# Decoder layer on one core: another order of instructions in a head pass, and a first pass with a program of its own

## The reference

```python
# 1: attention, 32 query heads and 8 key/value heads of 128 channels, int4 weights with a scale per 128 rows
w = (qw.astype(f32) - 8) * repeat(scales, 128, axis=0)
q, k, v = x @ w_q, x @ w_k, x @ w_v
q, k = rope(q), rope(k)        # t * cos + rotate_half(t) * sin
attn = softmax(causal(q @ k.T / sqrt(128)))
y = (attn @ v) @ w_o
# 2: attention to ctx, 16 heads of 32 channels, softmax over axis 0 of (batch * heads)
# 3: dense layer plus a two-of-eight LoRA mixture, gated by a small network
```

## Time and profile before

| | |
|---|---|
| Median of three runs | 731.64 us |
| The profiled execution, its own time | 731.3 us |
| Its span | 729.5 us |
| Mean granted TensorE clock | 0.978 |
| TensorE busy | 660.2 us, 90% |
| VectorE busy | 556.2 us, 76% |
| ScalarE busy | 452.6 us, 62% |
| GpSimd busy | 433.6 us, 59% |
| Phase -1 (first matmul of pass 0 to that of pass 1) | 11.93 to 38.03 us |
| Phase 0 | 38.03 to 66.92 us |
| Phases 1 to 14 | 66.92 to 479.0 us, 28.8 to 31.0 us each |
| Phase 15 and the last outs | 479.0 to about 505.6 us, then the other sublayers |

### The profile page before, as it was taken

The page is one execution under the profiler, slowest core; times in us unless marked ns, Lnnn a source line. Parts: engine busy times, 40 slices in busy tenths (PEclk is TensorE's granted clock), DMA queues, the critical chain, the costliest instruction groups (busy, mean ns, idle before and its releaser), DMA issues. The chain is left out here.

```text
span 729.5 us, 10970 instructions
## 1 busy us (share of the span) xinstructions
PE 660.2 (90%) x3297; PEld 448.2 (61%) x3298; DVE 556.2 (76%) x864; ACT 452.6 (62%) x1252; POOL 433.6 (59%) x379
## 2 busy tenths in 40 slices
PE   3579989999999999999999999978999889969994
PEld 2355867777778677677677777754554443348541
DVE  5756989899899898898898989955360359998446
ACT  2248859769788797796986976966233555412100
POOL 3759778888988988987998898852220000012002
PEclk9989999999999999999999999999999999979997
DMA  8344651441351242243144123130010000020003
GB/s 291 95 133 123 195 151 44 116 131 41 96 140 44 76 147 54 69 135 86 44 122 110 45 73 87 38 138 0 1 57 1 1 1 1 0 91 2 0 1 115
DMA packets 29469, 56.46 MB, mean 77 GB/s; under 512 B 4705, under 2 KB 4961, under 8 KB 28898
## 3 DMA queue, kind: packets, MB, share of 16 engines
q1 hardware_dynamic: 29410, 55.76, 26.9%
HBM read 32.67 MB, written 2.10 MB: 48 GB/s over the span
## 5 line engine op out<-in xcount | busy, mean ns | idle before, releaser
L943 DVE SCALAR_TENSOR_TENSOR arena<-ps,arena 128x512 f32<-128x512 f32 x288 | 213.5, 746 | 42.3 <-PE ps L1250 28.7
L1250 PE MATMUL ps<-x_hi,w_sb 128*128 128x512 f32 x384 | 176.1, 459 | 27.8 <-DVE x_lo L925 19.4
L971 DVE SCALAR_TENSOR_TENSOR y<-ps,arena,y 128x512 f32<-128x512 f32 x192 | 138.3, 742 | 28.8 <-PE ps L1309 28.7
L1250 PE MATMUL ps<-x_lo,w_sb 128*128 128x512 f32 x384 | 152.6, 397 | 0.0
L668 ACT ACTIVATE arena<-ps,arena 128x512 f32<-128x512 f32 x96 | 67.6, 704 | 98.7 <-PE ps L1250 88.2
L1309 PE MATMUL ps<-heads_hi,wo_sb 128*128 128x512 f32 x256 | 115.4, 451 | 7.3 <-DVE arena L943 3.0
L558 POOL TENSOR_TENSOR y<-arena,y 128x512 f32<-128x512 f32 x64 | 82.2, 1285 | 63.6 <-ACT arena L718 60.4
L540 POOL TENSOR_TENSOR arena<-arena,consts 128x512 f32<-128x512 f32 x80 | 103.5, 1294 | 27.2 <-DMA arena<-arena 25.6
L1250 PEld LDWEIGHTS ps<-x_hi,w_sb 128*128 128x128 f32 x384 | 73.3, 191 | 70.5 <-issue 34.0
L534 POOL TENSOR_TENSOR arena<-arena,consts 128x512 f32<-128x512 f32 x80 | 104.0, 1300 | 7.8 <-DVE arena L943 7.2
L550 POOL TENSOR_TENSOR arena<-arena 128x512 f32<-128x512 f32 x80 | 103.4, 1293 | 5.8
(11 more groups left out here) (117 smaller groups left out, 948.1 us busy)
## 6 DMA issues: line engine op xcount, KB each, us to landing
arena<-arena SPq DMA_DIRECT2D x160, 128.0 KB, 2.3
arena<-in_qkv SPq DMA_DIRECT2D x48, 256.0 KB, 3.7
arena<-in_o SPq DMA_DIRECT2D x32, 256.0 KB, 3.8
arena<-in_x_t SPq DMA_DIRECT2D x8, 256.0 KB, 5.6
y<-in_x SPq DMA_DIRECT2D x4, 512.0 KB, 4.2
arena<-in_ctx_t SPq DMA_DIRECT2D x4, 512.0 KB, 5.8
out<-y SPq DMA_DIRECT2D x8, 256.0 KB, 2.2
arena<-in_wk SPq DMA_DIRECT2D x1, 1024.0 KB, 5.9
```

What stands on the lines that cost most here:

```text
L943: nc.vector.scalar_tensor_tensor(acc, product_bank(f"G{KC * c + g}"), scale_of(p // 2, c, g), acc, ALU.mult, ALU.add).then_inc(dve_scaled, 1)
L971: nc.vector.scalar_tensor_tensor(dst, by_tile(out_bank(p, u)), out_scale_of(p // 2, u), dst, ALU.mult, ALU.add).then_inc(out_added, 1)
L1250: mm = nc.tensor.matmul(product_bank(f"G{u}"), w_sb[:, c, g, :], part[:, g, half * HALF:(half + 1) * HALF], start=(k == 0), stop=(k == 1))
```

## The change

1. **Order of a phase.** The lists of all four compute engines and `PRODUCTS` are rewritten. On TensorE O0 comes after three groups (six before), S0 after O0 and three more groups (and no longer after eight groups), V is after G2.2 (11th group), T0 before the tile 3 groups, S3 after T1, and the phase ends O13, O14, O15, W3 (before: O13, O14, W3, O15). VectorE's and ScalarE's lists follow. On GpSimd the weight conversions and outs lie elsewhere, and `cosine(2)` stands before `sine(2)`. The counts of operations stay the same.
2. **First pass.** x^T is loaded and cut chunk by chunk, each with its semaphore, and w tile 0 is loaded after chunk 0. ScalarE converts the first weights (before: GpSimd). ScalarE also makes `ident_b` and `mask_b` (before: VectorE, five small casts). The products of pass 0 go through seven banks in place of four. `raw_first`, `turned_first` and `cos_first` give every tile its own place (in the region of heads_hi and heads_lo), so no ring wait is left. VectorE's 18 additions go in the order `FIRST_SUMS`, which alternates tiles. Of the 15 rope operations GpSimd keeps eight and VectorE takes seven (sin and sum of tile 3, cos, sin and sum of tile 5, sin and sum of tile 4).
3. **Second half of x^T.** It is loaded after the turn of tile 0. VectorE makes its four x_lo between its last additions. ScalarE waits for `out_scales_in` only after phase 0.

```diff
@@ -52,8 +52,9 @@
 PRODUCTS = (
-    "G0 G1 G2 G3 G4 G5 O0 G6 G7 G8 O1 G9 G10 G11 O2 O3 G12 O4 O5 O6 G13 O7 G14 G15 G16 O8 O9 G17 O10 G18 G19 "
-    "G20 O11 O12 G21 G22 G23 O13 O14 O15").split()
+    "G0 G1 G2 O0 G3 G4 G5 G6 O1 G7 G8 G9 G10 G11 O2 O3 O4 O5 G12 O6 O7 O8 G13 G14 G15 O9 G16 G17 G18 G19 G20 "
+    "G21 O10 O11 G22 G23 O12 O13 O14 O15").split()
+FIRST_SUMS = "0.1 0.2 1.1 0.3 1.2 2.1 1.3 2.2 3.1 2.3 3.2 4.1 3.3 4.2 5.1 4.3 5.2 5.3".split()
 TURNS = "V T0 T1 T2 T3".split()
...
+        raw_first = carve(NT, HALF, base=HEADS_AT)
+        turned_first = carve(len(ROPE_TILES), HALF)
+        cos_first = carve(len(ROPE_TILES), HALF)
...
+        first_ps = [0, 1, 2, 7, 3, 4, 6]
...
+        def group_bank(p, u):
+            if p == 0:
+                return banks[first_ps[u % len(first_ps)]]
+            return product_bank(f"G{u}")
+        def raw_of(p, c):
+            return raw_first[:, c, :] if p == 0 else raw[:, c % RING, :]
+        def wait_group_read(eng, p, u):
...
+            def load_x(half, g):
+                sp.dma_start(x_stage[:, g, half * HALF:(half + 1) * HALF],
+                             t["x_t"][:, g, half * HALF:(half + 1) * HALF]).then_inc(x_in[half][g], 16)
+            def load_first_w(c):
+                sp.dma_start(w_int[:, c], t["qkv"][0][:, c]).then_inc(w_first_in[c], 16)
+            load_x(0, 0)
+            load_first_w(0)
+            for g in range(1, KC):
+                load_x(0, g)
             sp.dma_start(scales[:, :], t["qkv_scales"]).then_inc(scales_in, 16)
-            for c in range(1, NT):
-                sp.dma_start(w_int[:, c], t["qkv"][0][:, c]).then_inc(w_first_in[c], 16)
-                if c == 1:
-                    sp.dma_start(consts[:, :, :], t["consts"]).then_inc(consts_in, 16)
-            load_x(1)
+            load_first_w(1)
+            load_first_w(2)
+            sp.dma_start(consts[:, :, :], t["consts"]).then_inc(consts_in, 16)
+            for c in range(3, NT):
+                load_first_w(c)
...
-                    turn(p, c)
+            def turn_first(c):
+                wait(sp, dve_scaled, summed_count(0, c))
+                i = ROPE_TILES.index(c)
+                for a, b in ((0, 64), (64, 0)):
+                    sp.dma_start(turned_first[a:a + 64, i, :], raw_first[b:b + 64, c, :]).then_inc(first_turned_in[i], 16)
+            turn_first(0)
+            for g in range(KC):
+                load_x(1, g)
+            for c in ROPE_TILES[1:]:
+                turn_first(c)
             for k in range(QPK):
                 load_wo_piece(0, k)
...
@@ -588,19 +635,19 @@
                 cosine(0)
                 weights(0)
                 sine(0)
+                weights(1)
+                total(0)
+                cosine(2)
+                weights(2)
                 outs(3)
-                total(0)
                 sine(2)
-                cosine(2)
+                outs(7)
+                cosine(3)
                 total(2)
-                cosine(3)
-                outs(7)
-                weights(1)
+                weights(3)
                 sine(3)
                 total(3)
                 cosine(4)
-                weights(2)
-                weights(3)
                 sine(4)
                 cosine(5)
                 total(4)
@@ -608,14 +655,38 @@
                 total(5)
                 outs(11)
                 weights(4)
+                weights(5)
                 outs(15)
-                weights(5)
-            for c in range(NT):
-                wait(pool, w_first_in[c], 16)
-                convert(c)
             pool.wait_ge(consts_in, 16)
-            phase(-1)
...
+                nc.gpsimd.tensor_tensor(dst, cos_first[:, i, :], turned_first[:, i, :], ALU.add).then_inc(rotated, 1)
+            first_cos(0)
+            first_sin(0)
+            first_cos(2)
+            first_total(0)
+            first_sin(2)
+            first_cos(3)
+            first_total(2)
+            first_cos(4)
             phase(0)
...
+            def first_weights(c):
+                act.wait_ge(w_first_in[c], 16)
+                nc.scalar.activation(w_sb[:, c], w_int[:, c], ACT.Copy, bias=-ZERO).then_inc(w_ready, 1)
+            cut_x(0, 0)
+            first_weights(0)
+            for g in range(1, KC):
+                cut_x(0, g)
             act.wait_ge(scales_in, 16)
             def scale_group(p, c):
...
@@ -773,44 +850,62 @@
                 scale_groups(0)
                 scale_groups(1)
+                exp(0)
                 scale_groups(2)
-                exp(0)
-                exp(1)
                 seed(2)
                 norm(0)
+                copy_values()
+                exp(1)
                 outs(3)
+                seed(3)
+                copy_turned(0)
+                weights(0)
                 scale_groups(3)
-                copy_values()
-                seed(3)
+                outs(7)
+                exp(2)
                 norm(1)
-                copy_turned(0)
-                exp(2)
-                weights(0)
-                outs(7)
+                weights(1)
                 copy_head(0)
                 scale_groups(4)
+                norm(2)
+                seed(4)
                 copy_turned(1)
-                norm(2)
+                scale_groups(5)
                 exp(3)
                 copy_head(1)
                 copy_turned(2)
-                scale_groups(5)
+                norm(3)
                 outs(11)
-                norm(3)
+                weights(2)
                 copy_head(2)
-                seed(4)
                 copy_turned(3)
-                weights(1)
-                weights(2)
                 seed(5)
-                copy_head(3)
                 outs(15)
                 weights(3)
-            phase(-1)
-            cut_x(1)
+                copy_head(3)
+            first_weights(1)
+            scale_group(0, 0)
+            first_weights(2)
+            scale_group(0, 1)
+            act.wait_ge(consts_in, 16)
+            nc.scalar.activation(ident_b[:, :], ident, ACT.Copy).then_inc(mask_ready, 1)
+            first_weights(3)
+            scale_group(0, 2)
+            first_weights(4)
+            scale_group(0, 3)
+            first_weights(5)
+            copy_v(0)
+            scale_group(0, 4)
+            cut_x(1, 0)
+            cut_x(1, 1)
+            scale_group(0, 5)
+            cut_x(1, 2)
+            cut_x(1, 3)
+            nc.scalar.activation(mask_b[:, :, :], mask.unsqueeze(1).broadcast_to([P, QPK, P]), ACT.Copy).then_inc(mask_ready, 1)
+            phase(0)
             act.wait_ge(out_scales_in, 16)
-            for f in range(2 * NKV):
+            for f in range(1, 2 * NKV):
                 phase(f)
             act.wait_ge(params_in, 64)
...
@@ -996,41 +1087,79 @@
                     if f >= 0:
                         cut_heads(n + s)
-                add_groups(0, 1, 2, 3)
-                add_groups(1, 1, 2)
+                add_groups(0, 1, 2)
                 outs(0)
+                add_groups(0, 3)
+                add_groups(1, 1)
                 maximum(0)
+                add_groups(1, 2)
+                outs(1)
                 add_groups(1, 3)
+                inv(0)
                 maximum(1)
-                outs(1)
-                add_groups(2, 1)
-                inv(0)
-                add_groups(2, 2, 3)
+                add_groups(2, 1, 2, 3)
+                outs(2)
+                maximum(2)
+                outs(4, 5, 6)
                 inv(1)
-                outs(2, 4, 5, 6)
-                maximum(2)
+                outs(8)
                 add_groups(3, 1, 2)
-                maximum(3)
                 inv(2)
                 add_groups(3, 3)
+                outs(9)
                 cut(0)
-                outs(8)
                 add_groups(4, 1)
-                outs(9)
-                add_groups(4, 2)
+                maximum(3)
+                add_groups(4, 2, 3)
                 outs(10)
-                add_groups(4, 3)
+                add_groups(5, 1)
                 inv(3)
                 cut(1)
-                outs(12)
-                add_groups(5, 1, 2)
+                add_groups(5, 2, 3)
                 cut(2)
-                add_groups(5, 3)
-                outs(13, 14)
+                outs(12, 13, 14)
                 cut(3)
-            phase(-1)
-            cut_x(1)
...
+            for name in FIRST_SUMS[:13]:
+                first_sum(name)
+            cut_x(1, 0)
+            first_sum("4.2")
+            first_sum("5.1")
+            cut_x(1, 1)
+            first_sum("4.3")
+            first_sum("5.2")
+            cut_x(1, 2)
+            first_sum("5.3")
+            first_sin(3)
+            cut_x(1, 3)
+            first_total(3)
+            first_cos(5)
+            first_sin(4)
+            first_total(4)
+            first_sin(5)
+            first_total(5)
             phase(0)
             dve.wait_ge(y_in, 16 * BPH)
```

(69 more changed lines are left out.)

118 lines of the change are left out of this document (77 added, 41 removed).

## The result

The changed kernel takes 711.5 us (median of four runs, 709.9 to 712.4), and the kernel before took 731.8 us on the same chip: a ratio of 0.971, 95% interval 0.969 to 0.974. The prediction was 715.5 us, with a range of 702 to 726. The profiled execution took 712.35 us with a span of 710.6, so 18.9 us of span are to be found (729.5 - 710.6).

A forecast was written before the change was run, and what follows sets the result against it. TensorE was taken to bound a steady phase, the other engines close behind, with latencies setting phase 0. From 731.3 us, terms of -8, -1, -3.5, -2 and -1.5 gave 715.3, as a median 715.5 us; range 702 to 726.

The forecast's parts named there:

- term 1: First pass: VectorE's first addition of pass 1 starts near 34 against 42.07 us; -8.0 us, from -12 to 0.
- Rival A: First pass: all moved rope operations and x_lo collide with GpSimd's, so the start gains 0; 723.5 us, chance 0.15.
- term 2: Phase 0: GpSimd's chain some 2 us shorter, half of it counted; -1 us, from -2.5 to +1.
- Rival D: Start and steady phases: the early lead is lost before phase 1, phases keep their length; 731 +- 1 us, chance 0.03.
- term 3: Phases 1 to 14: fewer TensorE stalls, a mean gain of 0.25 us each; -3.5 us, from -15 to +7.
- small pieces: Steady phases: many small delays in TensorE's start times, some 0.5 us a phase, counted beside the named stalls.
- this walk: One steady phase of the new order followed by instruction distances: named stalls of 0.6 (odd) and 1.0 us (even).
- rival B: Phase boundary: W3 last puts W3, copy, cut and O0 across it, so O0 comes late; slower, 736 us, chance 0.09.
- Rival C: Steady phases: the new order fits far better than the walk, 1.0 us a phase; 705 us, chance 0.20.
- term 4: Single stalls of phases 2 and 10, 2.8 us: more than half goes; -2 us, from -3 to 0.
- term 5: Phase 15: the rope chain before its first scores starts 1.3 us earlier; -1.5 us, from -3 to +1.

The follow-up runs named there:

- d: The changed kernel with all 15 rope operations of the first pass on GpSimd: 712.7 us, ratio 0.972 to the kernel before.
- k: The changed kernel with 38 matmuls whose result nobody reads, placed where TensorE waits in phase 0: 709.2 us, ratio 0.970.
- l: The changed kernel with c, j, k (3 matmuls for 8 behind G3.0), late ctx loads, and odd phases' loads behind the last turn: 704.9 us.
- j: The changed kernel with head 1's weight loads issued between the turns of the first pass: 712.4 us, ratio 0.973.
- a: The changed kernel's first pass with the phase lists and product order of the kernel before: 723.2 us, ratio 0.987.
- c: The changed kernel with ScalarE reading G3.0 right after the second exponentials in phase 0: 710.0 us, ratio 0.970.
- h: The changed kernel with W3 back ahead of O15, and ScalarE's copy of heads 3 back ahead of out 15: 720.3 us, ratio 0.984.
- g: The kernel before with only O0 moved, behind three groups in place of six: 732.9 us, ratio 1.002.
- i: The changed kernel with S0 moved later, behind G1.3, and VectorE's maximum 0 and reciprocal moved to suit: 734.7 us, ratio 1.003.
- e1: The changed kernel with the four ctx loads issued near the end of the 16 passes: 708.9 us, ratio 0.970.
- b: The kernel before with the new phase lists and product order, its first pass otherwise as it was: 719.8 us, ratio 0.982.

## Why the prediction was right or wrong

**The start (term 1, -8.0; measured -8.9): right, by its mechanism.** The first addition was forecast near 10.3 and came at 10.21; the first of pass 1 near 34, and came at 33.18. Two errors offset each other in this: the thirteenth addition was over at 20.7 in place of 19.6, and two collisions in place of four gave back 2.1 us. The wait for the out scales is gone. (The 0.95 of phase -1, which I took for the slow first products, comes from its last 2.8 us; the slow start itself is there, in the distances.) Where two-input operations of both engines overlap they exclude each other (1.63 and 1.59 us from start to start against 0.75 and 0.6), as the Trainium skill says (SBUF — State Buffer, Who interferes with whom). Rival A took this rule as applying to all eleven; it needs both engines to be at it, and GpSimd had ended. Kernel d shows the other side: with the rope left to GpSimd, VectorE is free earlier and TensorE waits for GpSimd.

**Phase 0 (term 2, -1; measured +2.85): this step failed.** I reckoned with latencies of attention and rope that would stay or shrink. What I had not in the sum is the granted clock. Before, TensorE was at half clock from 35.2 and was back at full clock at 42.1, just when the first addition of pass 1 let it work. After, it works in spurts and the half clock lasts from 26.8 to 37.0, 3.9 us beyond the first addition, with another 3.4 us later. Kernels k and l show that this is the cause: at full clock the 24.85 us are back within 0.2. GpSimd's wait (j) is ruled out, and the new list adds at most 0.5 us (a). c, which only moves one read in ScalarE's list, gives back 1.7 us by itself and nothing on top of k: most of its gain, too, is a stretch of half clock that does not come. Rival D named the place (phase 1 no earlier than 60 us; it started at 60.87), but not this reason, and it held only for a third of the lead.

**The order of the phase (term 3, -3.5; measured about -11): right in sign, a term mis-sized threefold.** Undisturbed phases went from 29.25 to 28.0 us and from 28.8 to 28.5. The term that was mis-sized is what would be left of the stalls: I had 1.1 (odd) and 1.5 us (even), and what a phase takes beyond TensorE's own 27.45 is 0.55 and 1.05. O0 waiting for heads_lo, where I had 0.25 and 0.45 us and the traces show 0.17 and 0.19, is a smaller part of that; the rest is in the 0.5 us of small pieces and the bits at G1.1, W3 and O10. One reading in this walk was wrong, without weight: the W of the earlier trace rows ends at 185.42 and not at 185.26, so its copy follows after 0.03 us, not 0.2. The walk followed W3 to O0 as a risk, which rival B made its whole case. It did not follow what ScalarE does *while* W3 runs, nor how much longer an earlier W3 waits for its own input, and most of the gain needs these two: h, which undoes this alone, costs 1.1 us in odd phases, nearly the whole 1.25, and 0.5 in even ones, more than the 0.3. g shows that O0's place, my own reason, gives nothing by itself. The parts are not additive: i loses more than the whole gain by undoing S0's place alone. Rival C (1.0 us per phase) was the nearer for this term, which came out at 0.8. Rival B's sum leaves out my own gain of 3.5 us: the change would turn slower with O0 later by 16 / 14 = 1.14 us and not 0.9, and 1.2 us later gives 732.4, not 736.

**The single stalls (term 4, -2; measured about +2.3): this step failed.** I gave S0 a reserve of 1.1 us, with the last rope sum 2.6 us into the phase, and no loads in front of the turned tiles. In the kernel after this sum ends 3.1 to 3.2 us into the odd phases from 3 on. In even phases it ends at 3.8 and 3.9 us even where the tile is usable 3.2 and 3.3 us after its issue (phases 8 and 12), only 0.2 to 0.3 us ahead of S0. Where it takes 4.3 us (phases 4 and 10) it ends at 4.8, and with the ctx loads (phase 2) at 6.3. GpSimd in the kernel after, the last sums ahead of phases 4 and 8, which start at 149.35 and 263.83:

```profile
152.91 1.28 POOL L597 TENSOR_TENSOR arena<-arena 128x512 f32<-128x512 f32 x1
...
266.30 1.29 POOL L597 TENSOR_TENSOR arena<-arena 128x512 f32<-128x512 f32 x1
```

So S0 stalls 2.45, 0.64, 0.56 and 0.96 us in phases 2, 4, 6 and 10, where only 2 and 10 had a stall of their own before. For phase 2 e1 shows the cause, the ctx loads. For phases 4, 6 and 10 the cause beyond the thin reserve is open: transfers behind the same loads land at different times, from phase to phase and from run to run. That phase 2 grew more than its stall is again the clock (95.1 to 98.5 at half).

**Phase 15 (term 5, -1.5; measured -2.9): right, and larger.** The first scores of phase 15 in the kernel after, answering to the earlier trace rows:

```profile
466.12 1.13 PE L1397 MATMUL ps<-arena 128*128 128x128 f32 x8 [0.65 <-POOL arena L597]
```

They wait 0.65 us in place of 2.85; O0 ahead of them waits 1.4. The 1.3 us in the other two sublayers, which I had at 0, are most likely luck: the profiled execution after had 7.9 us at half clock there, the one before 21.9.

So two terms were too hopeful by 8 us together (2 and 4), and three too cautious by 10 (1, 3 and 5). That the total came within 4 us is in good part luck.

## What to carry to other kernels

An engine that is the bound can lose its clock while others catch up: when a change moves work of the others ahead, look where the bound engine idles in the new order, and price the same work at the lower clock (here 2.65 us of a lead of 8.9, given back in the trace by 38 matmuls that nobody reads). In lists that are taken in order, ask of each late instruction what its readers do while it runs, and what it waits for at the earlier place: W3 last gave ScalarE cover worth about 0.6 us in odd phases, and spared TensorE 0.3 to 0.5 us of waiting for W3's own input. Before an edit is credited with a stall that went away, look whether the stall is there in the other traces with the old code. A reserve that hangs on a small transfer is to be sized with the transfers ahead of it on its queue, and loads that nobody needs soon belong behind it.

## What the runs showed of the hardware that I had not expected

- The granted clock stays at 0.50 for 10.2 us (26.8 to 37.0) when TensorE works in spurts, 6.8 us in the kernel before, 13.7 in a, b, d and g. A stretch of 3.4 us of half clock came with single waits of 2.46 us (ending at 46.41) and 2.17 us (ending at 95.44).
- The two transfers of a turn (128 KB each, inside SBUF) are usable 2.9 us after their issue where no load was issued near them (the last turn ahead of phases 3 and 7), 3.2 to 4.3 us with two loads of 256 KB issued 2.2 to 2.8 us ahead and one behind, and 5.7 us with loads of 512 KB among them. One turn with two loads of 256 KB ahead took 3.1, so these loads don't always cost.
- A gain in the span of one profiled run may hardly show in the medians: c gained 3.6 us of span and 1.5 us of median, inside the intervals. Executions of one kernel differ with their mean granted clock: 17 of the kernel before took 728.98 us (clock 0.985) to 738.08 (0.971).
